# Forty multiplications of zeros ahead of TensorE's first step, in a decoder layer on one core

## The reference, cut to what matters

```
x = x + attn(layernorm(x), Wqkv, bqkv, Wout, bout)
x = x + xattn(layernorm(x), ctx, ctx, mask, Wq, bq, Wk, bk, Wv, bv, Wo, bo)
x = x + ffn(layernorm(x), Wp1, bp1, Wp2, bp2, W1, b1, W2, b2, Wo, bo)

def ffn(h, ...):
    sel = argmax(softmax(gelu(h[:, -1] @ Wp1 + bp1) @ Wp2 + bp2))
    y = gelu(h @ W1[sel] + b1[sel]) @ W2[sel] + b2[sel]
    return h + 0.3 * (y @ Wo + bo)
```

## Time and profile before

| | us |
|---|---|
| median of 3 runs | 1386.0 |
| lowest, highest | 1384.13, 1386.77 |
| the profiled execution | 1384.41 |
| its span, first to last instruction | 1382.7 |
| PE busy in it | 1337.8 (97%) |
| DVE busy | 1049.3 (76%) |
| granted TensorE clock, mean | 0.994 |

### The profile page before, as it was taken

How to read it: one execution, slowest core, us unless ns; L and a number is a source line. 1 busy time by engine, 2 the same in 40 slices (tenths; PEclk the granted TensorE clock), 3 DMA queues, 4 the chain that set the end, 5 groups by cost and what they waited for, 6 DMA issues and landing times.

```text
span 1382.7 us, 52798 instructions
## 1 busy us (share of the span) xinstructions
PE 1337.8 (97%) x23508; PEld 884.8 (64%) x23508; DVE 1049.3 (76%) x2191; ACT 667.3 (48%) x1228; POOL 570.3 (41%) x785
## 2 busy tenths in 40 slices
PE   8988999999999999999999999999999999999998
PEld 5765565765666666676666667666666667566555
DVE  3768788876778787877888787788778878688751
ACT  2423444544546454454636454564645454444552
POOL 6221444362534526363443526343452633534232
PEclk9999999999999999999999999999999999999999
DMA  8010300010202010020201101020101001001112
GB/s 286 2 33 3 111 17 35 3 54 8 62 10 61 10 45 27 7 64 3 61 11 44 28 30 42 2 62 10 45 27 45 20 2 42 29 18 39 44 58 65
DMA packets 54228, 54.17 MB, mean 39 GB/s; under 512 B 22370, under 2 KB 44146, under 8 KB 54002
## 3 DMA queue, kind: packets, MB, share of 16 engines
q1 hardware_dynamic: 45298, 42.42, 10.3%
q10 hardware_dynamic: 8704, 8.39, 1.8%
HBM read 37.16 MB, written 13.64 MB: 37 GB/s over the span
## 4 chain that ended last, share of the span: by engine, by line
PE 85%; DVE 8%; ACT 2%; issue 2%; DMA 1%; DVEq 1%; POOL 1%; POOLq 0%; SPq 0%; ACTq 0%
PE bank L1363 41%; PE bank L1610 8%; PE bank L1372 7%; PE bank L1382 7%; PE bank L1597 4%; PE bank L1434 2%; PE bank L1567 2%; PE bank L1576 2%; PE bank L1455 2%; PE bank L1488 2%; PE bank L1499 2%; PE bank L1595 1%; PE bank L1422 1%; DVE m_x L1222 1%; PE bank L1461 1%
## 5 line engine op out<-in xcount | busy, mean ns | idle before, releaser
L797 POOL TENSOR_TENSOR b<-ut,eye 128x256 f32<-128x256 f32 x192 | 137.6, 729 | 306.5 <-DVE ut L1191 180.2
L1363 PE MATMUL bank<-xnT_a,wqkv 128*128 128x512 f32 x256 | 119.1, 609 | 0.7 <-ACT xnT_a L883 0.7
L1182 DVE SCALAR_TENSOR_TENSOR wb<-bank,eye 128x256 f32<-128x256 f32 x192 | 72.9, 417 | 60.3 <-PE bank L1372 60.0
L1363 PE MATMUL bank<-w2e,hT 128*128 128x256 f32 x512 | 117.5, 383 | 0.9 <-ACT hT L1036 0.9
L1363 PE MATMUL bank<-xnT_c,w1e 128*128 128x512 f32 x256 | 116.9, 597 | 0.4 <-DMA b1e<-in_b 0.4
L1248 DVE RECIPROCAL oT_x<-bank 128x256 f32<-128x256 f32 x64 | 108.7, 1729 | 9.0 <-PE bank L1610 7.4
L1248 DVE RECIPROCAL oT<-bank 128x256 f32<-128x256 f32 x64 | 110.8, 1742 | 4.5 <-PE bank L1610 4.3
L1363 PEld LDWEIGHTS bank<-w2e,hT 128*128 128x128 f32 x512 | 96.7, 192 | 18.7 <-issue 6.5
L959 ACT ACTIVATE az<-bank 128x320 f32<-128x320 f32 x192 | 69.6, 406 | 74.9 <-PE bank L1372 73.0
L915 ACT ACTIVATE p3T<-bank 128x512 f32<-128x512 f32 x128 | 68.2, 601 | 60.3 <-PE bank L1488 54.7
L1222 DVE TENSOR_REDUCE m<-bank 128x8 f32<-128x512 f32 x128 | 82.8, 682 | 12.7 <-PE bank L1567 12.6
(11 more groups left out here) (226 smaller groups left out, 3039.9 us busy)
## 6 DMA issues: line engine op xcount, KB each, us to landing
x_in<-in_x SPq DMA_DIRECT2D x16, 512.0 KB, 4.3
w1e<-in_W SPq DMA_DIRECT2D x16, 512.0 KB, 4.1
w2e<-w2o SPq DMA_DIRECT2D x16, 512.0 KB, 3.3
out<-base ACTq DMA_DIRECT2D x32, 256.0 KB, 2.3
row_e<-w2o_row SPq DMA_DIRECT2D x16, 128.0 KB, 3.9
hT<-in_W2T SPq DMA_DIRECT2D x2, 512.0 KB, 7.8
pT_x<-in_ctxT SPq DMA_DIRECT2D x1, 1024.0 KB
vx<-pT SPq DMA_DIRECT2D x8, 128.0 KB, 1.9
```

The costliest lines, as they stand in the source:

```text
L797: return g.tensor_tensor(b7[i % 2][:, q, :], ut[i % 2][:, q, :], eye[28 if it else 7][:].unsqueeze(1) .broadcast_to([P, 4, LM]), ALU.subtr ...
L1182: return v.scalar_tensor_tensor(wb[i % 2][:, h], src, 1.0 / 16 if it else 1.0, eye[15][:].unsqueeze(1).broadcast_to([P, 4, LM]), ALU.mult, ...
L1363: last = mm(dst, lhsT, rhs, start=(k == 0), stop=(k == len(pairs) - 1))
```

## The change

A DVE memset writes zeros into the first 128 columns of `x1`, ahead of DVE's first step. PE waits for it and then multiplies that 128x128 block by itself forty times, into the first 128 columns of the last bank, ahead of its wait for `pool_consts` and of its first step. Nothing reads the products; the bank's first real user overwrites them.

```
+        zeros_ready = sem("zeros_ready")
...
         @block.vector
         def _(dve):
             v = nc.vector
+            v.memset(x1[:, 0, 0:P], 0.0).then_inc(zeros_ready, 1)
+
             def statistics(x, src, tiles=range(T)):
...
         @block.tensor
         def _(pe):
             mm = nc.tensor.matmul
+            pe.wait_ge(zeros_ready, 1)
+            for _ in range(40):
+                mm(banks[BANKS - 1][:, 0:P], x1[:, 0, 0:P], x1[:, 0, 0:P], start=True, stop=True)
             if first(pe, pool_consts, 1):
                 pe.wait_ge(pool_consts, 1)
```

## The result

The changed kernel takes 1398.24 us (median of 6 runs, 1392.76 to 1400.11) against 1385.94 for the kernel before (6 runs): 1.0087 times as long, 95% interval 1.0076 to 1.0099. The forecast was 1389.5, its range ended at 1391.8. So the sign was right, and the size, +12.3 us instead of +3.5, was not. The profiled execution took 1397.0, its span is 1395.3, 12.6 more than before.

A forecast was written before the change was run, and what follows sets the result against it. PE was taken as the bound, busy 97% of the span. The blocks, less gains at the higher clock, move `hT` from 12.55 to 16.05 us: +3.5 on the median of 1386.0 gives 1389.5 us, range 1386.6 to 1391.8.

The forecast's parts named there:

- The blocks: Head of PE's queue: forty multiplications make 80 records, 0.217 us each at low clock, then 0.109, ending at 11.7 us.
- The low stretch at the start: PE's first work, on the zeros: 1.2 GHz for 3.9 us, or 18 records, with 3.4 and 6.8 us as ends.
- the ends: Alternative shifts of step `hT`: +3.2 us with 3.4 us of low clock at the start, +4.9 with 6.8.
- Does it last to the end?: After the start, through the whole run: no later gap takes up the delay, so +3.5 us arrives at the end whole.
- The gap at 72.6: PE's first gap after 60 us, 2.7 us, ended by DVE: moves to about 76 with its length kept, absorbing nothing.
- rival D: Later low-clock stretches, 17.0 us, go as PE's stream shifts; all of it would give 1381.0 us; 4%.
- Rival C: PE's start: zeros don't raise the clock, the blocks take 17.4 us, `fb` starts 12.3 us later, 1398.3 us; 5%.
- Rival A: PE's start: each block is one record, not two, so they end at 7.35 us; 1385.1 us; 6%.
- rival B: From 72 us on, PE's waits on something PE doesn't drive take up 2 us or more; 1387 or less; 6%.
- The page's figure: 56 ns per 128-column record would make the blocks 6.4 us and the shift -0.8 us; set aside for the trace's 0.109.

The follow-up runs named there:

- without any blocks: Kernel before, PE's first step waiting for 14 or 17 ACT copies onto scratch instead of any added multiplications: 1388.77 (ratio 1.0022) and 1389.45 us (1.0037).
- forty tiny blocks: Changed kernel with its forty multiplications each cut to an 8x1 block, 160 PE instructions: 1388.80 us against 1386.17 for the kernel before, ratio 1.0026.
- 34 and 30: Changed kernel with 34 full multiplications and 30 of 8x1 in place of forty full, 256 PE instructions: 1388.47 us, ratio 1.0028 to the kernel before.
- 64 tiny blocks: Kernel before plus 64 multiplications of 8x1, 256 PE instructions: 1385.13 us against 1385.01, ratio 0.9989.
- the tiny blocks and the load moved: Forty 8x1 multiplications, with SP's load of x for the last batch moved behind two small loads: 1390.22 us, ratio 1.0030 to the kernel before.

## Why the prediction was wrong

**The blocks.** 80 records, 0.213 and 0.112 us apart where I had 0.217 and 0.109, no wait on the weight loads: right. The low stretch at the start was 4.9 us, I had taken 3.9 and named 3.4 to 6.8. With a gap of 0.2 us before `fb`, 0.1 before `f.4`, and the blocks' start at 1.12 instead of 1.05, the step `hT` was at +4.55 instead of +3.5, inside the ends (+3.2 to +4.9). This term was mis-sized by 1 us, half of it by the longer low stretch.

**Does it last to the end?** That the delay arrives whole is shown: +2.6 for +3.0 and +5.3 for +5.0 without any blocks, +4.3 for +4.5 with them. The gap at 72.6 did not take it up; it was 0.4 us shorter (2.3 against 2.7), with the forty tiny blocks, which delay nothing, as well. The step that failed is the sentence that followed: "So +3.5 us arrives at the end whole", as if with it nothing else would arrive. I had counted what the 160 instructions take to execute and not that they are instructions, which move every later one by 160 places in blocks of 256. I had put that term at nothing without a reason. It costs 2.6 us without any delay (forty tiny blocks against none) and 4.4 us at the same delay (the changed kernel against 34 and 30), and at a multiple of 256 nothing (64 tiny blocks; 34 and 30). The rows were there to be seen: two of PE's waits near 150 us had "issue" as their releaser.

The late packets do not cost by PE's waits for them alone: these sum to 5.0 us in the changed kernel's first trace, to 2.4 in its second and to 1.8 with the tiny blocks and the load moved, against 2.5 before. The traces show a second path, which I had overlooked. All six traces with 160 more instructions have it, one of the other eleven does (twelve blocks). It runs through a store of the result near 1313 us before, near 1323 in the changed kernel. The DMA views of before, 1312.5 to 1316.5 us, and of the changed kernel, 1323.4 to 1327.4, show the store:

```profile
out<-base ACTq DMA_DIRECT2D x1, 256.0 KB, 2.7
...
out<-base ACTq DMA_DIRECT2D x1, 256.0 KB, 4.1
```

In the seven traces an instruction packet of PE starts 0.9 to 2.2 us after the store's issue, while the store runs, and the store's last packet arrives after 3.5 to 4.3 us; in the other ten the instruction packet starts after 2.6 us or more, and the store is through after 2.2 to 2.8. POOL waits for that store before its next two steps. The timelines of POOL and DVE, 1317 to 1321 us before, then 1329 to 1333 in the changed kernel:

```profile
1317.78 2.34 POOL L718 TENSOR_TENSOR base<-base,row_e 128x1024 f32<-128x1024 f32 x1
1318.58 1.59 DVE L1233 CAST m_parts_x<-m_x 128x64 bf16<-128x64 f32 x1
1320.24 0.23 DVE L1235 TENSOR_TENSOR m_rest_x<-m_x,m_parts_x 128x64 f32<-128x64 f32 x1
...
1329.53 0.62 DVE L1236 CAST m_parts_x<-m_x 128x64 bf16<-128x64 f32 x1
1330.17 2.34 POOL L719 TENSOR_TENSOR base<-base,row_e 128x1024 f32<-128x1024 f32 x1
1330.22 2.37 DVE L1238 TENSOR_TENSOR m_rest_x<-m_x,m_parts_x 128x64 f32<-128x64 f32 x1
```

DVE's instruction ends with POOL's, however short it is elsewhere: before, 0.8 us of POOL's step had passed when DVE's began, and in the changed kernel DVE meets all of it. PE's waits for the result, 1300 to 1345 us, before and in the changed kernel:

```profile
PE bank L1583 <- DVE m_parts_x L1239: 1.2, 1, 1.2
...
PE bank L1589 <- DVE m_parts_x L1242: 2.4, 1, 2.4
```

This wait lasts 2.0 to 2.8 us in the seven traces and 1.0 to 1.3 in the ten. In each of the seven a low stretch of 3.4 us starts within 1 us of its end (in the changed kernel the one at 1333.85), in none of the ten. By these rows it is worth some 1.2 + 1.7 = 2.9 us, an estimate. No run isolates it.

**The low clock.** I gave rival D, that the later low stretches change, only its good side, and 4%. The stretches changed, the other way: in the six sets of runs with 160 instructions added the mean low clock was 28.4, 23.2, 22.2, 23.7, 22.9 and 20.4 us, in the eight others with blocks or a delay 16.6 to 20.4, and in the kernel before 17.8 to 20.2. The sets overlap, but their means do not: 23.2 us over 48 runs, 17.9 over 79 and 19.4 over 95. Half of the difference between each set and the kernel before beside it, 0.2 to 3 us in five sets and 4 to 5 in the first, is part of the loss. Where it comes from is only in part to be seen: one stretch behind the wait near 1330 us, and in two traces a fall within a microsecond of the end of a fetch wait. It does not all follow from the fetch waits, since both traces of the changed kernel have 10.2 us more than the first trace of before ahead of the first of them. Such early stretches change from trace to trace in every kernel (3.4 to 10.2 us before 205 us in the eleven traces without the 160 instructions). No run keeps the waits and the clock apart. It stays open too why the first six runs of the changed kernel lie 3.6 us further off than the next six.

**Rival C** stood at 1398.3 and the result is 1398.24; it was nevertheless false. Zeros do raise the clock, at 6.06 us. The agreement is chance. **Rival A** (one record each) and **rival B** (slack takes it up) did not occur.

**The page's figure** of 56 ns per 128 columns, from the Trainium skill's "TensorE: Matmul & The Clock Gate", section "Back-to-back issue gap", was set aside for the trace's 0.109; 0.112 was measured for float32. That section gives the 56 ns for an isolated multiplication, and about 81 ns at 128 columns for a stream of weight loads and multiplications, which the blocks are; no run here shows either.

## What to carry to other kernels

Before a warm-up is put ahead of an engine's first step, look at what the step after it waits for: here PE would have waited for a load anyway, so even the right number of blocks won nothing that could be measured, and forty overran the idle time by 6 us. In a long unrolled program, adding instructions to the busiest engine is a change of its own. Look for waits whose releaser is "issue", count their place in the engine's instructions, and try the change with a filler that makes the added count a multiple of the fetched block before judging it. And do not close a sum with the waits that one looked for: add up all gaps of the engine, and look at the ones that grew.

## What the hardware showed that I had not expected

PE can run out of instructions in the middle of a step: 2.8 to 3.1 us at one place, up to 1.7 us at others, always at the same remainder of 256, and it goes on 1.2 to 1.6 us after an instruction packet has arrived. Most of these places are where short multiplications follow each other (256 instructions in 3 to 7 us), but the longest wait is not. With an instruction packet started in the middle of it, a store of 256 KB was through after 3.5 to 4.3 us in place of 2.2 to 2.8. A DVE instruction of 0.23 us took 2.37 beside a step of POOL. Adding 160 instructions that take 2.15 us in an idle stretch cost 2.6 us at the end; adding 256 cost nothing.
